# The last layer normalisation of both halves on ScalarE instead of VectorE

## What is computed

```python
def _layernorm(x, axis=-1, eps=1e-5):
    m = jnp.mean(x, axis=axis, keepdims=True)
    v = jnp.var(x, axis=axis, keepdims=True)
    return (x - m) / jnp.sqrt(v + eps)
...
x = _layernorm(x + _L0_gnn_ref(x, adj, ...))     # hypergraph convolution, 512 -> 1024 -> 512
x = _layernorm(x + _L1_gnn_ref(x, adj, ...))     # pairwise weights exp(8 tanh(.)), then A @ x @ w
x = _layernorm(x + _L2_gnn_ref(x, adj, ...))     # three graph convolutions
x = _layernorm(x + _L3_gnn_ref(x, nodemask, adj, adj, ...))   # attention with 8 heads
```

## Time and profile before

| | us |
|---|---|
| median of 3 runs | 2669.83 (2668.64 to 2670.15) |
| the profiled execution | 2667.08 |
| its span, first to last instruction | 2665.1 |
| TensorE busy | 2590.1 (97%) |
| VectorE busy | 1856.3 (70%) |
| ScalarE busy | 893.6 (34%) |
| GpSimd busy | 469.0 (18%) |

### The profile page before, as it was taken

How to read it: one execution, slowest core, us unless ns; L and a number is a source line. 1 busy time by engine, 2 the same in 40 slices (tenths; PEclk the granted TensorE clock), 3 DMA queues, 4 the chain that set the end, 5 groups by cost and what they waited for, 6 DMA issues and landing times.

```text
span 2665.1 us, 74512 instructions
## 1 busy us (share of the span) xinstructions
PE 2590.1 (97%) x30297; PEld 2183.5 (82%) x30297; DVE 1856.3 (70%) x4168; ACT 893.6 (34%) x2796; POOL 469.0 (18%) x746
## 2 busy tenths in 40 slices
PE   7999999999999999999999999999999999999998
PEld 5788888887888888788888888888888888888887
DVE  5888888888888888866655665764665665566565
ACT  3222222222222222343432432433333243243333
POOL 1222222222222222210110111011011011101101
PEclk9999999999999999999999999999999999999999
DMA  3211111111111111311101101101110110110100
GB/s 129 83 39 39 39 40 39 39 39 39 39 39 39 39 39 39 115 32 35 36 15 31 35 19 29 35 19 32 35 31 16 35 35 15 31 35 19 29 20 17
DMA packets 128229, 100.87 MB, mean 38 GB/s; under 512 B 86676, under 2 KB 88744, under 8 KB 127912
## 3 DMA queue, kind: packets, MB, share of 16 engines
q1 hardware_dynamic: 125872, 95.18, 11.6%
q10 hardware_dynamic: 2040, 1.13, 0.1%
HBM read 62.68 MB, written 33.55 MB: 36 GB/s over the span
## 4 chain that ended last, share of the span: by engine, by line
PE 86%; DVE 7%; ACT 3%; issue 2%; POOL 2%; DMA 0%; ACTq 0%; DVEq 0%; POOLq 0%
PE ps L1317 23%; PE ps L631 18%; PE ps L1302 14%; PE ps L1320 11%; PE ps L634 9%; PE ps L623 4%; PE ps L1344 3%; PE ps L1382 1%; PE ps L1357 1%; PE ps L1389 1%; POOL sm L261 1%; DVE sm L480 1%; POOL sm L263 1%; DVE sm L478 1%; ACT Fp L351 1%
## 5 line engine op out<-in xcount | busy, mean ns | idle before, releaser
L1174 DVE TENSOR_TENSOR Tl<-ps,Th 128x256 fp32r<-128x256 f32 (+1 forms) x576 | 227.7, 446 | 88.9 <-ACT Th L1100 74.7
L987 POOL TENSOR_TENSOR Fp<-Fp,mhalf 128x1 f32<-128x1 f32 x128 | 78.6, 614 | 1175.2 <-DVE Fp L1181 1175.2
L631 PE MATMUL ps<-W1h,Th 128*128 128x512 f32 x512 | 205.9, 402 | 1.9 <-DVE Tl L453 1.8
L631 PE MATMUL ps<-W2h,Th 128*128 128x512 f32 x512 | 203.9, 398 | 3.1 <-DVE Tl L488 1.1
L631 PE MATMUL ps<-W1l,Th 128*128 128x512 f32 x512 | 200.8, 392 | 0.0
L631 PE MATMUL ps<-W2l,Th 128*128 128x512 f32 x512 | 199.9, 390 | 0.0
L1105 ACT ACTIVATE R<-R 128x512 f32<-128x512 f32 x128 | 80.9, 632 | 352.2 <-DVE R L1215 352.2
L1129 ACT ACTIVATE E<-E,Fp 128x64 f32<-128x64 f32 x512 | 170.8, 340 | 32.5 <-DVE Fp L1249 31.3
L261 POOL TENSOR_SCALAR sm<-sm 128x1 f32<-128x1 f32 x192 | 78.9, 411 | 557.8 <-DVE sm L482 298.9
L1241 DVE COPY QK<-ps 128x512 f32<-128x512 f32 x64 | 44.1, 689 | 166.7 <-PE ps L1302 166.7
L1302 PE MATMUL ps<-Th,Wh 128*128 128x256 f32 x512 | 147.7, 288 | 0.0
(11 more groups left out here) (208 smaller groups left out, 6657.2 us busy)
## 6 DMA issues: line engine op xcount, KB each, us to landing
X<-in_x SPq DMA_DIRECT2D x64, 256.0 KB, 6.3
x<-R SPq DMA_DIRECT2D x64, 256.0 KB, 2.4
X<-x SPq DMA_DIRECT2D x64, 256.0 KB, 2.7
out<-E SPq DMA_DIRECT2D x64, 256.0 KB, 2.1
AB<-in_adj SPq DMA_DIRECT2D x504, 8.0 KB, 1.7
NX<-in_adj SPq DMA_DIRECT2D x128, 32.0 KB, 2.2
E<-in_L_W1T SPq DMA_DIRECT2D x8, 256.0 KB, 6.8
E<-in_L_W SPq DMA_DIRECT2D x4, 512.0 KB, 5.1
```

Source lines behind the costliest of these rows:

```text
L631: pe.matmul(out, Th[:, c, j * P:(j + 1) * P], R(j), start=(j == 0 and R is Rh), stop=False)
L1174: return dve.tensor_tensor(lo, ps, hi.bitcast(F32), ALU.subtract)
```

## The change

The operation `(x - mean) * rstd` of steps `x2` and `x4` moves from VectorE to ScalarE, as `Identity(rstd * x + bias)` with two per-partition columns as scale and bias. VectorE now writes the bias `-mean * rstd` into a new column NM (one element in each partition) and raises a new semaphore `nm_ok`, for which ScalarE waits. `x2_ok` and `x4_ok`, which release the stores, are raised by ScalarE. `ORDER`, `START`, `TRANSITION` and `END` are unchanged, so ScalarE's part stands in its queue where the step always stood. To free a semaphore, `cols_ps` is merged into `v_ps` (set-up only, the counts waited for rise by one).

```diff
-    VE, RS, S, RI, CI = range(5)
+    VE, RS, S, RI, CI, NM = range(6)
...
-        sp.wait_ge(v_ps, scaled_pieces + 1)
+        sp.wait_ge(v_ps, scaled_pieces + 2)
...
+        def x2_norm(c, n):
+            act.wait_ge(nm_ok, n[c])
+            act.activation(R[:, c, 0:D], R[:, c, 0:D], ACT.Identity, bias=col(c, NM), scale=col(c, RS)).then_inc(x2_ok, 1)
...
+                if step == "x2":
+                    x2_norm(c, n)
...
         def x2_norm(c, n):
             dve.wait_ge(rs3, n[c])
-            dve.tensor_scalar(R[:, c, 0:D], R[:, c, 0:D], col(c, MV), col(c, RS), ALU.subtract, ALU.mult).then_inc(x2_ok, 1)
+            dve.scalar_tensor_tensor(col(c, NM), col(c, MV), -1.0, col(c, RS), ALU.mult, ALU.mult).then_inc(nm_ok, 1)
...
+                    if step == "x4":
+                        act.wait_ge(nm_ok, done + n[c])
+                        act.activation(Z[c % 2], Z[c % 2], ACT.Identity, bias=col(c, NM), scale=col(c, RS)).then_inc(x4_ok, 1)
...
                     if step == "x4":
                         dve.wait_ge(rs4, done + n[c])
-                        dve.tensor_scalar(Z[c % 2], Z[c % 2], col(c, MV), col(c, RS), ALU.subtract, ALU.mult)\
-                            .then_inc(x4_ok, 1)
+                        dve.scalar_tensor_tensor(col(c, NM), col(c, MV), -1.0, col(c, RS), ALU.mult, ALU.mult).then_inc(nm_ok, 1)
```

More of the change, by code:

```diff
@@ L48 @@
     later early bias12 v_all wa_all NX CU Fp ps consts_ok ident0 vec_in load_in split_hi split_lo pieces x_in norm1 norm2 later_in at_ok cur_ok h_ok S_ps bias_ok u_ok s_ok b1_B r_psB y2_ps y3_ps z1 z2
-    x2_ok x2_stored""")
+    x2_ok nm_ok x2_stored""")
 handed_over = []
@@ L117, in hypergraph_and_pairwise @@
     consts_ok, ident0, b2_half = sem("consts_ok"), sem("ident0"), sem("b2_half")
-    vec_in, cols_ps, cols_sb, split_hi, split_lo, v_ps, v_sb = map(sem, (
-        "vec_in", "cols_ps", "cols_sb", "split_hi", "split_lo", "v_ps", "v_sb"))
+    vec_in, cols_sb, split_hi, split_lo, v_ps, v_sb = map(sem, ("vec_in", "cols_sb", "split_hi", "split_lo", "v_ps", "v_sb"))
     load_in = [sem(f"load_in{i}") for i in range(KD + KH // 2 + 2)]
@@ L129, in hypergraph_and_pairwise @@
      r_psA, r_psB, b1_A, b1_B, r_sbA, r_sbB, bn1, mv1, ve1, rs1, rc_ok, g2_ok, t2_psA, t2hA, t2hB,
-     t2_sb, y2_ps, z1, bn2, mv2, ve2, rs2, x1_ok, s_ok, sb_ps, tanh_ok, lrelu_ok, exp_ok,
+     t2_sb, y2_ps, z1, bn2, mv2, ve2, rs2, x1_ok, s_ok, sb_ps, tanh_ok, lrelu_ok, exp_ok, nm_ok,
      af_ok, t3_ps, t3h, ri_ok, t3_sb, y3_ps, z2, bn3, mv3, ve3, rs3, x2_ok) = map(sem, (
@@ L134, in hypergraph_and_pairwise @@
         "r_psA r_psB b1_A b1_B r_sbA r_sbB bn1 mv1 ve1 rs1 rc_ok g2_ok t2_psA t2hA t2hB "
-        "t2_sb y2_ps z1 bn2 mv2 ve2 rs2 x1_ok s_ok sb_ps tanh_ok lrelu_ok exp_ok "
+        "t2_sb y2_ps z1 bn2 mv2 ve2 rs2 x1_ok s_ok sb_ps tanh_ok lrelu_ok exp_ok nm_ok "
         "af_ok t3_ps t3h ri_ok t3_sb y3_ps z2 bn3 mv3 ve3 rs3 x2_ok").split())
@@ L372, in columns @@
         def columns():
-            act.wait_ge(cols_ps, 1)
+            act.wait_ge(v_ps, 1)
             act.copy(vec_cols[:, :], psB[CH - 1][:, 0:2 * KH + KD]).then_inc(cols_sb, 1)
         def products_with_vectors():
-            act.wait_ge(v_ps, scaled_pieces)
+            act.wait_ge(v_ps, scaled_pieces + 1)
             act.mul(v_all[:, :], psB[CH - 1][:, :], 0.5).then_inc(v_sb, 1)
-            act.wait_ge(v_ps, scaled_pieces + 1)
+            act.wait_ge(v_ps, scaled_pieces + 2)
             act.mul(wa_all[:, :], psB[CH - 1][:, :], 0.125).then_inc(v_sb, 1)
@@ L684, in columns @@
             pe.wait_ge(vec_in, 5 * 16)
-            pe.transpose(psB[CH - 1][:, 0:2 * KH + KD], vec_rows[:, :], ident[0:2 * KH + KD, 0:2 * KH + KD]).then_inc(cols_ps, 1)
+            pe.transpose(psB[CH - 1][:, 0:2 * KH + KD], vec_rows[:, :], ident[0:2 * KH + KD, 0:2 * KH + KD]).then_inc(v_ps, 1)
         def beta_product(v):
@@ L738, in hypergraph_and_pairwise @@
         later, early, bias12, v_all, wa_all, NX, CU, Fp, ps, consts_ok, ident0, vec_in, load_in, split_hi, split_lo, len(pieces), x_in, (bn1, mv1, ve1, rs1), (bn2, mv2, ve2, rs2), later_in, at_ok, cur_ok, h_ok, S_ps, bias_ok, u_ok, s_ok, b1_B, r_psB, y2_ps, y3_ps, z1, z2,
-        x2_ok, x2_stored))
+        x2_ok, nm_ok, x2_stored))
 HEADS, DHEAD = 8, 64
@@ L802, in convolutions_and_attention @@
                [[odd(W, c, i) for W in (Th, Tl)] for c in (1, 3) for i in range(2)])
-        MC, VE, RS = range(3)
+        MC, VE, RS, NM = range(4)
         MV, BN, NMX, NB, SUM, REC, RLA = 4, 8, 16, 24, 32, 40, 48
@@ L833, in convolutions_and_attention @@
         b_ok = [sem(f"b_ok{i}") for i in range(2)]
+        nm_ok = first.nm_ok
         t_ps, th, t_sb, g_ps, g_sb = ([sem(f"{n}{i}") for i in range(3)] for n in ("t_ps", "th", "t_sb", "g_ps", "g_sb"))
```

## The result

| | before | after |
|---|---|---|
| median, us | 2669.36 (2668.64 to 2670.15, 4 runs) | 2714.35 (2712.43 to 2716.06, 4 runs) |
| the profiled execution, us | 2667.08 | 2714.49 |
| its span, us | 2665.1 | 2712.5 |

The changed kernel is slower by a ratio of 1.0169 (95% interval 1.0153 to 1.0185), 45.0 us in the medians and 47.4 us in the profiled spans. The forecast was 2715, a sum of +46.75.

What follows compares the result with a forecast made beforehand. TensorE, busy 97% of the span, was taken as the bound. Terms 21 + 9.75 + 12 + 1.5 + 2 + 0.5 = 46.75 us on the profiled 2667.08 gave 2714, stated as 2715 for the median; range 2692 to 2732.

Steps and rivals of the forecast that it cites:

- The durations: Prices taken: 0.82 us for a normalisation on ScalarE, 0.16 us for the bias on VectorE.
- Place A: x2.0 in the first-half loop, ahead of t3e.2 and S: TensorE's tx.0 1.4 us late, 15 times, 21 us.
- Place B: x2.1 and x2.2 in the first-half loop, ahead of t2e.0's casts: TensorE's y2.1 0.65 us late, 15 times, 9.75 us.
- the 1.2 given as a sign: Sign of place B: VectorE idle 1.2 us for the cast of t2e.0, right behind two small operations.
- Place C: x4.0 in the second-half loop, ahead of t0.0's cast: TensorE's g0.0 0.8 us later, 15 times, 12 us.
- x4.1: Second-half loop, ahead of ta.3's copy and t0.1's casts: slot does not quite fit, 0.1 us, 15 times, 1.5 us.
- x2.3, x4.2 and x4.3: Other normalisations in the two loops: idle time or later need covers them, so they cost TensorE nothing.
- Joint and end: TRANSITION between the halves, x2.3 and x2.0 there: 2 us; last x4 at the program's end: 0.5 us.
- A is covered: Rival: tx.0 late by half of the forecast or not at all, 2693 to 2704 us; chance 0.13.
- The stalls lower TensorE's clock: Rival: each stall of place A costs 1.3 us more through the clock, +20, 2734 us; chance 0.05.
- Relief of VectorE decides: Rival: no one waits behind x2 and x4 on ScalarE, so 17 us less, 2650 us; chance 0.04.
- No change: Rival: costs and relief cancel as VectorE makes up the loss later, 2662 to 2672 us; chance 0.04.

Runs made afterwards that it cites:

- wait_only: Kernel before, VectorE normalising everywhere; in the first half ScalarE only waits at x2.0 for VectorE's result: 2686.23 us, +16.7 over before.
- free_places: Changed kernel, everything on ScalarE, with x2.0, x2.1, x2.2, x4.0 at other list places, also some at joint and end: 2670.39 us against 2670.2 before.
- x20_alone: Kernel before with only x2.0 (tile 0 of the first half) moved to ScalarE: 2692.98 us, +23.7 over before.
- b_alone: Kernel before with only x2.1 and x2.2 (tiles 1 and 2 of the first half) moved to ScalarE: 2678.23 us, +8.7 over before.
- c_behind_sm: Changed kernel with x4.0 behind the exponentials of sm.3 in ScalarE's second-half loop list: 2706.6 us, 7.8 less than the changed kernel.
- a_behind_S: Changed kernel with x2.0 behind the copy of S in ScalarE's first-half loop list: 2688.51 us, 25.8 less than the changed kernel.

## Why the prediction was right, and where it was not

- **ScalarE's low busy share is no room at the place where the step stands.** Shown by `wait_only` (no work, +16.7 us). Other stretches of its idle time are room, as `free_places` shows (all the work, no loss).
- **The durations.** 0.815 and 0.152 us for the 0.82 and 0.16 taken. The bias comes 0.19 us ahead of ScalarE's start (790.92 to 791.11), as forecast (0.20).
- **Place A, 1.4 us a group.** The mechanism was as told, the size a little low: TensorE idles for 1.47 us (from 792.38), the period of `x20_alone` grows by 1.57, and its 23.7 us over the 15 groups of the loop are 1.58 each. (The sixteenth `x2.0` stands at the joint and costs nothing, 145.06 us against 145.09.) From VectorE's small operation to `tx.0` the forecast had 2.78 us (766.57 to 769.35), the trace has 2.92 (790.92 to 793.84). The slot is 0.84 us and not 0.72, because the operation and the cast behind it did not overlap; from the copy of `S` to GpSimd it is 0.22 and not 0.12; the rest is 0.08 shorter. GpSimd's copy took 0.29 us, which is the short value that the 1.4 was made with.
- **Place B, 0.65 us.** The size was right, 0.61 us in the chain and 8.7 us in `b_alone` for 9.75. The step that failed is the route: "z1.0 starts 0.65 us later ... y2.1 waits". VectorE did stand idle ahead of L493, for 1.99 us (the 1.2 given as a sign does not fit the prediction's own times either, which make it 2). Behind that it worked without a gap up to `z1.0`. The 0.66 us of idle time of before took `z1.0`'s delay down to 0.55, but they lie behind the statistics of tile 2, from which GpSimd (L262) and then `gs.2` on ScalarE follow; that chain kept 1.30 us of delay and was the first to be late for TensorE. The prediction had given `gs.2` the low bound, 0.3. That `gs.2` is the releaser is read from the trace; no run took it away alone.
- **Place C, 0.8 us.** That cast and normalisation now stand one behind the other was right; that `x4.0` was "already in the chain of waits" was not, and so the term was mis-sized: 0.52 us in a typical group, 7.8 us in `c_behind_sm` for 12. The group at 1780 us that gave the numbers is the one of 15 in which `rs4.0` was late, so `x4.0` was in the chain there, and 0.29 us of slack was missing. In that group the forecast 0.8 was right. "The groups repeat within hundredths of a us" was wrong, and that sentence is the step that failed.
- **x4.1, 0.1 us.** Nothing: TensorE's gap there is 0.08 us after and 0.11 before. The two errors of the second half are 4.2 us for C and 1.5 here; its loop came out 5.3 below the forecast.
- **x2.3, x4.2 and x4.3, nothing.** TensorE has no new wait in a group beside those of A, B and C.
- **The first half was forecast 5 us too low** (35.9 with its first period, 30.75): 14 periods grew by 2.3 and not by 2.05, and the first by 3.5. Of the 2.3 place A has 1.57 for 1.4 and place B 0.77 for 0.65: both cost TensorE more than the idle time of the stall (below). Place A costs 2.75 in the first period; why more than later is open.
- **Joint and end.** 1.6 for 2, and none of it is of `x2.0` (`x20_alone`). The end cost 1.15 for 0.5; 0.9 of it is TensorE's clock in one execution and not the change, as the section on the hardware shows, and some 0.3 are left.
- **Why the sum came out.** Too little for the first half (5) against too much for the second (5.3). The value is better than its terms.
- **The rivals.** "A is covered" fell with `x20_alone`. "The stalls lower TensorE's clock": the granted clock is 0.997 over the span and 1.00 from 200 to 900 and from 1300 to 2500 us. At the end it was lower than before, but `a_behind_S`, with the same end, had it in full there. "Relief of VectorE decides": `free_places` shows the relief without the waits, and it brings nothing, because TensorE has only some 0.6 us of idle time in a group of 67.0 before, and 1.7 in one of 96.0. "No change" fell with the result.

The Trainium skill's rule (ScalarE: Activation LUTs, Rules for kernel authors) that additions and multiplications belong to VectorE holds here for the operation, 0.54 against 0.815 us. It does not decide the kernel: with it broken 128 times at other places of the list, no time is lost.

## What to carry to other kernels

Idle time of an engine that works its list in order can be an instruction's wait with ready work behind it; before work is put there, read what stands behind the place, in that list and behind every store that the work releases, and ask when the input comes. The cheap places here were those behind what the bounding engine waits for next, and moving one entry of one engine's list was worth 25.8 us here with the same work. And look at several groups before a sum is made from one: whether the operation was on the chain hung on 0.3 us, and one group of 15 said yes.

## What the runs showed of the hardware

**The overlap is not always there.** ScalarE's operations in a row mostly start 0.1 us before the one ahead ends. At place A the cast began only behind the end of the normalisation (791.11 + 0.82 = 791.93 and 791.95), and so in all 15 groups. The wait ahead of the normalisation is not the reason: at place B it had waited too, for 0.61 us, and two normalisations took 1.52 us together and the cast began 0.10 us before their end; at place C it had waited 0.69 us, and the cast began at 1629.47 with its end at 1629.56. What makes place A different is open.

**GpSimd's copy is slow only beside VectorE's normalisation.** Of before (minimum/median/maximum):

```profile
L270 POOL COPY CU<-NX x64: 288/298/487, 17.0 to 1068.3; 128x132 f32<-128x132 f32 x64
```

The 0.49 us copy of the earlier trace rows ran beside L540. Of the 64 copies 15 took 483 to 487 ns, and they are the ones beside L540; no other took over 301. The mean is 341 ns before; after it is 294 and in `free_places` 296, where L540 is gone, and in `wait_only`, where VectorE still normalises but the copy comes later, 296 too. The Trainium skill (SBUF — State Buffer, SBUF: two separate sides) has a port that VectorE and GpSimd share and that one of them holds for a whole operation. The trace agrees that the two hinder each other, by 0.19 us; that is less than the 0.33 us for which the copy ran beside L540 (766.78 to 767.11), so here the copy was not held up for all of it.

**The clock at the end.** The last twelve wide products, first of before, then of after, then of `a_behind_S` (stretch, length, busy time and instructions of PE, PEld, DVE, ACT and POOL, granted clock, DMA share, GB/s):

```profile
2654.60:2659.10 4.50, 4.50 (x12) 3.27 (x12) 1.80 (x5) 0.00 (x0) 0.55 (x1) 0.62 0.00 0
```

```profile
2700.80:2706.20 5.40, 5.40 (x12) 3.77 (x12) 1.81 (x5) 0.00 (x0) 0.55 (x1) 0.50 0.00 0
```

```profile
2675.40:2678.30 2.90, 2.90 (x12) 2.07 (x12) 1.74 (x5) 0.00 (x0) 0.55 (x1) 1.00 0.00 0
```

After, the granted clock is 0.50, the lower level (1.2 GHz), over the whole of them; before, it was 0.62, between the levels. Ahead of them, in the three us from 2651 and from 2697, TensorE was busy for 1.35 us in both kernels. The twelve take 5.47 us for 4.58, 0.9 us, and that is most of the 1.15 of the end. In `free_places` they take 5.47 us too. But the change does not set this. `a_behind_S` has the same end as after, and there the twelve took 3.00 us at a granted clock of 1.00; in `b_alone`, whose end is that of before, they took 2.98. So the same products at the end took between 3.0 and 5.5 us, by the clock that one execution had there, and the spans of two single profiles can differ by so much without a change of the kernel. What decides where the clock changes is open.

**A stall costs more than its idle time.** TensorE's busy time in after is 9.7 us higher with the same 30297 products. From 200 to 900 us it is 692.16 us before, or 66.25 in a period of 67.0, and 672.79 after, or 66.6 in one of 69.3: about 0.35 us a group for two stalls, with the granted clock at 1.00 in both. Where the stalls are gone (`free_places`) it is 692.13 again. Products in a row overlap: before, `tx.0` started 0.99 us after the start of the four products ahead of it (766.96 to 767.95), though these ran to 768.03. At a stall the last product runs to its end alone. At place A it is 2.53 us after, 1.54 more for 1.47 of idle time; at place B it is 3.33 us from the start of the products of L628 to `y2.1` for 2.62, 0.71 more for 0.61. In the second half, where the stall only grew, the busy time does not rise (94.2 and 94.1 a period).
